# A conv block with a mixture-of-experts tail: a weight load on another queue, choices counted by matmuls, and work around them reordered

## The chip, the cores and the metric

The kernel runs on one core of a Trainium2 chip. The metric is the device time of one execution in microseconds (us). Engines are called PE (matrix), ACT (scalar), DVE (vector), POOL (GpSimd) and SP (sync, which only issues transfers here).

## The reference, cut to what matters

The input is 8 images of 16x16 pixels and 192 channels, 2048 tokens in all. Stage 1 is a layer norm over channels, then 28 correlations of each pixel's unit vector with neighbours along four lines, then a 1x1 convolution over 192 + 28 channels, added to the input. Stage 2 is a layer norm and a top-2 mixture of 8 experts with a capacity:

```python
x = x + _L0_conv_ref(_ln_c(x), conv_w, conv_b)      # features and 28 correlations, 1x1 conv
t = _to_tokens(x)
t = t + _L0_ffn_ref(_ln_t(t), Wg, W1, W2)

# in _L0_ffn_ref, for each of the 2 choices k:
onehot = ik[:, None] == jnp.arange(E)[None, :]
pos = jnp.cumsum(onehot, axis=0) - 1                # a token's place in its expert's list
keep = posk < capacity                              # 307 places
h = jnp.einsum('ecd,edh->ech', xg, W1)
act = h[..., :H] * jax.nn.silu(h[..., H:])
ye = jnp.einsum('ech,ehd->ecd', act, W2)
```

The place of a token in its expert's list depends on all earlier tokens, so stage 2 can start its first expert only when the last token has chosen.

## The kernel before, in words

All orders are written out by hand: each engine has its own block, the engines run their lists in order, and semaphores join them. Stage 1 works on four groups g of 512 tokens (4 tiles of 128). Where the sources below name a call such as `turn_f(2)`, the number is the group.

For a group, in the order of the data: DVE takes mean and variance (`stats`), ACT the square roots (`deviation`), DVE the scales (`scales`), ACT writes normalized features f (`features`), PE transposes them (`turn_f`, lines 980 and 981), ACT copies the result to SBUF (`take_features`), PE forms products of neighbouring pixels (`grams`, lines 1002 and 1003, in two halves), ACT copies them out (`take_gram`), SP stores them to DRAM and reads them back skewed (`gram_round`), POOL picks the 28 correlations (`correlations`, line 454), PE transposes those (`turn_corr`, line 1013), ACT copies them (`take_corr`, tile ct) and PE does the convolution with the router's columns beside it (`conv_features`, line 1026; `conv_rest`, line 1033).

Then DVE has the longest list. `combine` makes router scores (lines 749 and 751), `choose` takes the two best experts and a one-hot tile (lines 775 to 791), `residual` adds the convolution (line 757), `stats_b` takes the second norm's statistics (lines 766 and 769), `find_slots` turns counted places into slots (lines 797 to 806), `row_scales` makes scale and shift of the second norm (lines 811 to 815) and `spots` (lines 822 to 828) makes the tiles from which PE builds a table of tokens by slot (`fill_table`, line 1077). ACT writes the normalized rows (`normed`, line 565), SP stores them to DRAM (`store_rows`, lines 380 and 381) and the residual output (`store_x1`, line 371). Counting is done on PE in `places`: a strictly upper triangular matrix `before` counts within a tile, `ones` counts whole earlier tiles of the group, and `seen`, a running sum that DVE keeps, counts earlier groups.

After group 3 DVE turns the table into row numbers (`indices`, line 840 gives `source`), and POOL, which waits first for `source_ready` and then for all row stores (`rows_out`), gathers the rows of experts 0 and 1 (line 480). Each expert is then a block of matmuls on split operands (lines 1150 to 1158, 1173, 1175), some 18 us, with PE busy nearly throughout. Weights of an expert are four transfers, 1.4 MB: `load_w1` (three, lines 310 to 312) and `load_w2` (line 316). Experts 0 and 1 are loaded by ACT's queue, the others by SP's.

`keep_busy(n, ...)` on PE is a filler: n matmuls of 512 columns whose result nobody reads (line 967). It stands at the start (20), ahead of `turn_corr(0)` (`BUSY_FIRST`, 7), ahead of `turn_corr(3)` (6), between `places(3)` and `fill_table(3)` (`BUSY_TABLE`, 14) and behind `fill_table(3)` (24).

Of the kernel before, what the change touches and what calls it, by code (L numbers as in the profile page):

```python
# [31 lines left out]
BF16 = mybir.dt.bfloat16  # L32
# [90 lines left out]
def metaformer_kernel(nc, x, conv_wt, conv_w, wg, w1, w2, consts, out):  # L123
# [4 lines left out]
    with ExitStack() as ctx:  # L128
# [71 lines left out]
        onehot = sb("onehot", [P, TILES, TOPK, E], BF16)  # L200
        seen = sb("seen", [P, GROUPS, TOPK * E], BF16)
        chosen = sb("chosen", [P, TOPK * E])
# [63 lines left out]
        seen_ready = sem("seen_ready"); shift_ready = sem("shift_ready"); slot_ready = sem("slot_ready")  # L266
# [67 lines left out]
        def _(sp):  # L334
# [75 lines left out]
        def _(pool):  # L410
# [5 lines left out]
            G.memset(seen[:, 0, :], 0.0)  # L416
# [89 lines left out]
        def _(s):  # L506
# [175 lines left out]
        def _(v):  # L682
# [89 lines left out]
            def choose(g):  # L772
# [3 lines left out]
                then(last)  # L776
                for t in range(TILES):
                    last = V.max_index(top_e[:, t, :], top[:, t, :], score[:, t, :])
                then(last)
                if g >= 1:  # L780
                    v.wait_ge(spots_ready, g)
                V.tensor_tensor(onehot[:, :, :, :],
# [4 lines left out]
                if g + 1 < GROUPS:  # L787
                    v.wait_ge(choice_ready, g + 1)
                    then(V.tensor_reduce(chosen[:, :], onehot[:, :, :, :].rearrange("p t k e -> p (k e) t"),
                                         AX_X, ALU.add))  # L790
                    V.tensor_tensor(seen[:, g + 1, :], seen[:, g, :], chosen[:, :], ALU.add).then_inc(seen_ready, 1)

            def find_slots(g):

                picks = slice(g * TILES * TOPK, (g + 1) * TILES * TOPK)
                v.wait_ge(place_done, g + 1)
                then(V.tensor_tensor(place_e[:, :, :],
                                     bank[7][:, 0:TILES * TOPK * E].rearrange("p (n e) -> p n e", e=E),
                                     onehot[:, :, :, :].rearrange("p t k e -> p (t k) e"), ALU.mult))
# [8 lines left out]
            def row_scales(g):  # L808
# [147 lines left out]
        def _(pe):  # L956
# [95 lines left out]
            def places(g):  # L1052

                if g == 0:
                    pe.wait_ge(before_ready, 1)
# [156 lines left out]
```

## Time and profile before

| what | us |
|---|---|
| median of 3 runs (lowest, highest) | 230.23 (229.35, 232.94) |
| the profiled execution, its own time | 229.77 |
| its span in the trace | 228.0 |
| stage 1, to the first gather | about 62.7 |
| eight experts, to the end | about 159 |
| PE busy, share of the span | 205.2, 90% |

### The profile page before, as it was taken

The numbers are of one execution on the slowest core, as the hardware profiler recorded it, in microseconds if no ns is written. First come the engines' busy times: TensorE is split into PE (matmuls) and PEld (weight loads), VectorE is DVE, ScalarE is ACT, GpSimd is POOL, SyncE is SP. The second block draws the span as 40 slices with busy tenths as digits, with TensorE's granted clock in tenths as the row PEclk, the third lists the DMA queues.
The fourth block names the chain that finished last, engine by engine and source line by source line (L and its number), as shares of the span: only waits on it lengthen the run. The fifth ranks groups of instructions, "written<-read, shape, count | busy, mean of one in ns | idle before, by whom it ended". The sixth has DMA issues, their size and how long they took to land.

```text
span 228.0 us, 4487 instructions
## 1 busy us (share of the span) xinstructions
PE 205.2 (90%) x1351; PEld 188.3 (83%) x1351; DVE 160.2 (70%) x509; ACT 128.3 (56%) x320; POOL 118.7 (52%) x130
## 2 busy tenths in 40 slices
PE   7998799869858999999999999999999999999930
PEld 2786699653327999999999999999999999999920
DVE  2674989998704599598598678679778868956520
ACT  2454765374202476587578578577568658745510
POOL 5102212100077154885877787687687683185184
PEclk9999999976795899999999999999999999999995
DMA  6648375879724392494395386288278253034043
GB/s 206 183 123 236 69 204 164 188 195 294 169 73 105 69 289 66 68 286 98 43 262 132 56 252 135 52 175 212 55 139 236 69 52 31 0 36 49 0 46 42
DMA packets 28015, 29.40 MB, mean 129 GB/s; under 512 B 6915, under 2 KB 24544, under 8 KB 28000
## 3 DMA queue, kind: packets, MB, share of 16 engines
q1 hardware_dynamic: 18656, 17.28, 26.6%
q0 software_dynamic: 7680, 9.05, 23.7%
q10 hardware_dynamic: 1664, 2.88, 4.8%
q8 instruction: 7, 0.11, 0.2%
q14 instruction: 8, 0.07, 0.1%
HBM read 19.86 MB, written 9.35 MB: 128 GB/s over the span
## 4 chain that ended last, share of the span: by engine, by line
PE 71%; DVE 11%; DMA 7%; POOL 3%; ACT 3%; issue 2%; SPq 1%; POOLq 0%; DVEq 0%; ACTq 0%
PE low L1173 6%; PE bank L1173 5%; PE first L1157 4%; PE first L1154 4%; PE first L1150 4%; PE first L1158 4%; PE first L1151 4%; PE low L1157 4%; PE low L1158 4%; PE low L1154 4%; PE low L1151 4%; PE low L1150 4%; PE both L1173 3%; PE low L1175 2%; PE bank L1175 2%
## 5 line engine op out<-in xcount | busy, mean ns | idle before, releaser
L500 POOL DMA_INDIRECT out<-y,goal x40 | 65.9, 1648 | 36.6 <-DVE y L933 27.4
L480 POOL DMA_INDIRECT rows<-rows_dram,source x40 | 42.5, 1062 | 36.2 <-DMA rows_dram<-row 18.9
L902 DVE TENSOR_TENSOR al<-act,ah 128x308 fp32r<-128x308 f32 x64 | 30.1, 471 | 1.0
L635 ACT CAST ah<-act 128x308 fp32r<-128x308 f32 x64 | 28.3, 443 | 1.8 <-DVE act L910 1.8
L910 DVE TENSOR_TENSOR act<-low,sil 128x308 f32<-128x308 f32 x32 | 15.3, 479 | 12.8 <-ACT sil L642 12.8
L642 ACT ACTIVATE sil<-first 128x308 f32<-128x308 f32 x32 | 13.7, 428 | 16.7 <-PE first L1158 15.6
L642 ACT ACTIVATE sil<-low 128x308 f32<-128x308 f32 x32 | 13.7, 428 | 14.2 <-PE low L1158 13.3
L910 DVE TENSOR_TENSOR act<-first,sil 128x308 f32<-128x308 f32 x32 | 15.3, 479 | 8.0 <-ACT sil L642 7.2
L1150 PE MATMUL first<-xh_a,hi_a 128*128 128x308 f32 x64 | 20.1, 314 | 0.7 <-ACT xh_a L625 0.7
L1157 PE MATMUL first<-x_b,hi_b 128*128 128x308 f32 x64 | 20.1, 314 | 0.0
L1154 PE MATMUL first<-xl_a,hi_a 128*128 128x308 f32 x64 | 19.9, 312 | 0.1
L1158 PE MATMUL low<-x_b,lo_b 128*128 128x308 f32 x64 | 19.9, 311 | 0.0
L1158 PE MATMUL first<-x_b,lo_b 128*128 128x308 f32 x64 | 19.9, 311 | 0.0
L1157 PE MATMUL low<-x_b,hi_b 128*128 128x308 f32 x64 | 19.9, 311 | 0.0
L1151 PE MATMUL low<-xh_a,lo_a 128*128 128x308 f32 x64 | 19.8, 309 | 0.0
L1151 PE MATMUL first<-xh_a,lo_a 128*128 128x308 f32 x64 | 19.8, 309 | 0.0
L1154 PE MATMUL low<-xl_a,hi_a 128*128 128x308 f32 x64 | 19.8, 309 | 0.0
L1150 PE MATMUL low<-xh_a,hi_a 128*128 128x308 f32 x64 | 19.6, 307 | 0.0
L1173 PE MATMUL low<-w,ah 128*128 128x384 f32 x64 | 19.4, 368 | 0.0
L1173 PE MATMUL bank<-w,ah 128*128 128x384 f32 (+1 forms) x64 | 19.2, 356 | 0.0
L1175 PE MATMUL low<-w,al 128*128 128x192 f32 x64 | 16.0, 251 | 0.0
L967 PE MATMUL first<-ones 128*128 128x512 bf16 x51 | 14.8, 457 | 1.3 <-POOL conv_b L417 1.3
(172 smaller groups left out, 562.3 us busy)
## 6 DMA issues: line engine op xcount, KB each, us to landing
raw_b<-w SPq DMA_DIRECT2D x12, 256.0 KB, 4.1
raw_a<-w SPq DMA_DIRECT2D x6, 512.0 KB, 5.3
raw<-w SPq DMA_DIRECT2D x6, 384.0 KB, 6.1
gram_dram<-gram SPq DMA_DIRECT2D x8, 230.0 KB, 3.2
xt<-x_tokens SPq DMA_DIRECT2D x4, 384.0 KB, 4.4
out<-xt SPq DMA_DIRECT2D x4, 384.0 KB, 5.1
rows_dram<-row SPq DMA_DIRECT2D x3, 386.0 KB, 4.3
raw_b<-w ACTq DMA_DIRECT2D x4, 256.0 KB, 4.2
```

Of the source, the lines that this page charges most:

```text
L480: G.indirect_dma_start(out=rows[b][:, t, :], out_offset=None, in_=rows_dram, in_offset=bass.IndirectOffsetOnAxis(ap=source[:, n:n + 1], ax ...
L500: nc.gpsimd.indirect_dma_start(out=out, out_offset=bass.IndirectOffsetOnAxis(ap=goal[0:m, n:n + 1], axis=0), in_=y[0:m, t, :], in_offset=N ...
L635: nc.scalar.copy(ah[:, j, lo:hi], act[n % 3][:, 0:hi - lo]).then_inc(a_hi, 1)
L642: nc.scalar.activation(sil[n % 2][:, 0:hi - lo], bank[2 * (n % 2) + 1][:, 0:hi - lo], ACT.Silu).then_inc(sil_ready, 1)
L902: V.tensor_tensor(al[:, j, lo:hi], act[n % 3][:, 0:hi - lo], ah[:, j, lo:hi].bitcast(F32), ALU.subtract).then_inc(a_lo, 1)
L910: V.tensor_tensor(act[n % 3][:, 0:hi - lo], bank[2 * (n % 2)][:, 0:hi - lo], sil[n % 2][:, 0:hi - lo], ALU.mult).then_inc(act_ready, 1)
L1150: T.matmul(o, hi_a[b][:, cols], xh_a[:, lo:hi], start=True, stop=False)
L1151: T.matmul(o, lo_a[b][:, cols], xh_a[:, lo:hi], start=False, stop=False)
L1154: T.matmul(o, hi_a[b][:, cols], xl_a[:, lo:hi], start=False, stop=False)
L1157: T.matmul(o, hi_b[b][:, cols], x_b[:, lo:hi], start=False, stop=False)
L1158: mm = T.matmul(o, lo_b[b][:, cols], x_b[:, lo:hi], start=False, stop=True)
L1173: T.matmul(acc, ah[:, j, cols], w_2[b][:, j, :, :].rearrange("p h n -> p (h n)"), start=(j == 0), stop=(j == NH - 1))
```

## The change

Seven things are done. The counting on DVE (`chosen`, `seen`) goes, and `places` counts earlier groups by matmuls of `ones` with the one-hot tiles of those groups, which are now kept apart (one per group); 4, 8 and 12 such matmuls for groups 1, 2 and 3. In `places` they stand first, behind a wait for `slot_ready`, and the `before` matmul stands last. The 7 fillers ahead of `turn_corr(0)` go. On ACT both halves of `take_gram(1)` come ahead of `deviation(3)` and `take_corr(0)`, and `load_w1` of expert 0 comes behind them, directly ahead of `features(2)`. `turn_corr(1)` moves between the halves of `grams(2)`. On ACT `take_corr(3)` moves ahead of `deviation_b(2)`. The weights of expert 1 are issued by SP behind the last row store in place of ACT behind `normed(2)`, and `store_rows(2)` stands ahead of `store_x1(1)`. On DVE the last group takes `residual` and `stats_b` first, then the best scores, then `row_shifts`, and only then `max_index`, the one-hot tile and the rest.

```diff
@@ sync
             store_x1(0)
+            store_rows(2)
             store_x1(1)
-            store_rows(2)
             store_x1(2)
             store_rows(3)
+            load_w1(sp, 1, 1)
+            load_w2(sp, 1, 1)
             store_x1(3)
@@ scalar
             deviation(2)
+            take_gram(1)
+            deviation(3)
+            take_corr(0)
             load_w1(s, 0, 0)
-            take_gram(1, (0,))
-            take_corr(0)
-            deviation(3)
-            take_gram(1, (1,))
             features(2)
...
+            take_corr(3)
             deviation_b(2)
-            take_corr(3)
             normed(2)
-            load_w1(s, 1, 1)
-            load_w2(s, 1, 1)
@@ vector, choose
-                if g + 1 < GROUPS:
-                    v.wait_ge(choice_ready, g + 1)
-                    then(V.tensor_reduce(chosen[:, :], onehot[:, :, :, :].rearrange("p t k e -> p (k e) t"),
-                                         AX_X, ALU.add))
-                    V.tensor_tensor(seen[:, g + 1, :], seen[:, g, :], chosen[:, :], ALU.add).then_inc(seen_ready, 1)
@@ vector, the groups
                 else:
-                    row_scales(g)
+                    residual(g)
+                    stats_b(g)
+                    best_scores(g)
+                    row_shifts(g)
+                    choose(g)
+                    row_gaps(g)
                     find_slots(g)
@@ tensor, places
+                if g >= 1:
+                    pe.wait_ge(slot_ready, g)
+                for p in range(g):
+                    for t in range(TILES):
+                        T.matmul(o, ones[:, :],
+                                 onehots[p][:, t, :, :].rearrange("p k e -> p (k e)").unsqueeze(1).broadcast_to([P, TILES, TOPK * E]),
+                                 start=(p == 0 and t == 0), stop=False, skip_group_check=True)
                 pe.wait_ge(choice_ready, g + 1)
...
                 if g >= 1:
-                    pe.wait_ge(seen_ready, g)
-                    pe.wait_ge(slot_ready, g)
-                T.matmul(o, ones[:, :], seen[:, g, :].unsqueeze(1).broadcast_to([P, TILES, TOPK * E]),
-                         start=False, stop=True).then_inc(place_done, 1)
+                    last = T.matmul(o, before[:, :], picks, start=False, stop=True, skip_group_check=True)
+                last.then_inc(place_done, 1)
@@ tensor, the program
             grams(1)
-            keep_busy(BUSY_FIRST, bank[0])
             turn_corr(0)
             conv_rest(0)
             turn_f(2)
             places(0)
-            grams(2)
+            grams(2, (0,))
             turn_corr(1)
+            grams(2, (1,))
             conv_features(1)
```

On DVE, the last group before, from its scores to its slots (score holds the router's scores, top and top_e the best ones and their experts, xt the tokens, mv_b the second norm's mean and variance):

```order
L751 TENSOR_TENSOR score<-both,part 128x32
L775 MAX top<-score 128x8 x4
L778 MAX_INDEX top_e<-top,score 128x8 x4
L782 TENSOR_TENSOR onehot<-cst,top_e 128x64
L786 TENSOR_TENSOR gap<-top 128x4
L757 SCALAR_TENSOR_TENSOR xt<-both,norm,xt 128x192 x4
L766 BN_STATS stat_b<-xt 128x6 x4
L769 BN_AGGR mv_b<-stat_b 128x2 x4
L811 RECIPROCAL rstd_b<-sd_b 128x4
L812 SCALAR_TENSOR_TENSOR shift_b<-mv_b,rstd_b 128x4
```

And the same place in the changed kernel:

```order
L747 TENSOR_TENSOR score<-both,part 128x32
L753 SCALAR_TENSOR_TENSOR xt<-both,norm,xt 128x192 x4
L762 BN_STATS stat_b<-xt 128x6 x4
L765 BN_AGGR mv_b<-stat_b 128x2 x4
L771 MAX top<-score 128x8 x4
L804 RECIPROCAL rstd_b<-sd_b 128x4
L805 SCALAR_TENSOR_TENSOR shift_b<-mv_b,rstd_b 128x4
L777 MAX_INDEX top_e<-top,score 128x8 x4
L779 TENSOR_TENSOR onehot<-cst,top_e 128x64
L783 TENSOR_TENSOR gap<-top 128x4
```

The one-hot tile, for which `places(3)` on PE waits, moves behind shift_b, for which ACT's `normed(3)` waits.

On PE, the end of stage 1 in the changed kernel (low and bank are PSUM tiles; the filler is `first<-ones` or `low<-ones`):

```order
L1086 MATMUL bank<-tile_e,lane_e 128x40 x8
L1065 MATMUL bank<-onehot,ones 128x64 x12
L1074 MATMUL bank<-onehot,ones 128x48
L1074 MATMUL bank<-onehot,ones 128x32
L1074 MATMUL bank<-onehot,ones 128x16
L1077 MATMUL bank<-onehot,before 128x64
L970 MATMUL low<-ones 128x512 x14
```

Before, the twelve matmuls were not there and one with `seen` stood last; the 14 fillers stood behind the counting in both.

On ACT, the front before, from the second group's features to the third group's:

```order
L513 ACTIVATE len_a<-mv_a 128x4
L310 DMA raw_b<-w 64x1024
L311 DMA raw_b<-w 64x1024
L312 DMA raw_a<-w 128x1024
L549 COPY gram<-low 128x358
L554 COPY ct<-bank 93x512
L512 ACTIVATE sd_a<-mv_a,eps_c 128x4
```

And in the changed kernel:

```order
L548 COPY gram<-low 128x358 x2
L511 ACTIVATE sd_a<-mv_a,eps_c 128x4
L512 ACTIVATE len_a<-mv_a 128x4
L553 COPY ct<-bank 93x512
L308 DMA raw_b<-w 64x1024
L309 DMA raw_b<-w 64x1024
L310 DMA raw_a<-w 128x1024
L523 ACTIVATE f<-xt,shift_a,q_a 128x192 x4
```

The three weight transfers moved from ahead of the copies to a place directly ahead of `features(2)`.

## Rows read from the trace of the kernel before

**Rows 1.** The page, granted TensorE clock in 40 equal slices of the span.

```profile
PEclk9999999976795899999999999999999999999995
```

**Rows 2.** Windows: stretch, length, busy of PE, PEld, DVE, ACT, POOL, clock, DMA share, GB/s.

```profile
18.30:25.80 7.50, 5.16 (x34) 3.53 (x32) 4.14 (x32) 4.12 (x11) 1.68 (x7) 1.00 0.67 178
44.00:49.00 5.00, 2.26 (x13) 1.72 (x12) 4.69 (x23) 2.62 (x6) 0.00 (x0) 1.00 0.71 168
49.00:57.00 8.00, 7.30 (x27) 3.78 (x27) 7.22 (x41) 3.92 (x10) 0.00 (x0) 0.58 1.04 283
59.00:63.00 4.00, 4.00 (x13) 1.53 (x13) 3.22 (x8) 0.00 (x0) 0.31 (x1) 0.57 0.57 109
69.00:77.00 8.00, 7.34 (x32) 6.77 (x31) 3.22 (x7) 2.56 (x6) 5.08 (x5) 0.57 0.40 99
```

**Rows 3.** Timeline of PE, 18 to 26 us: start, duration, then the instruction.

```profile
18.28 1.67 PE L967 MATMUL first<-ones 128*128 128x512 bf16 x7
19.79 0.60 PE L1013 MATMUL bank<-cst,fc 128*93 128x128 f32 x4
21.06 1.67 PE L1033 MATMUL both<-conv_b,ct 93*128 93x208 f32 x8 [0.67 <-ACT ct L554]
23.55 0.30 PE L980 MATMUL first<-cst,f 128*128 128x128 f32 x1 [0.81 <-ACT f L524]
...
25.77 0.57 PE L1002 MATMUL low<-ft_a 128*128 128x179 f32 x2 [0.79 <-ACT rows L538]
```

**Rows 4.** Timelines of ACT and POOL in the same stretch.

```profile
15.09 0.61 ACTq L310 DMA_DIRECT2D raw_b<-w  x1
...
20.43 0.58 ACT L554 COPY ct<-bank 93x512 f32<-93x512 f32 x1 [2.70 <-PE bank L1013]
...
21.54 1.86 ACT L524 ACTIVATE f<-xt,shift_a,q_a 128x192 f32<-128x192 f32 x4
...
18.19 0.89 POOL L454 TENSOR_TENSOR fc<-near,picked 128x28 f32<-128x28 f32 x4 [4.34 <-DMA near<-gram_dram]
```

**Rows 5.** Timeline of DVE, groups 0, 1 and 3 and the indices.

```profile
24.57 0.26 DVE L789 TENSOR_REDUCE chosen<-onehot 128x16 f32<-128x64 bf16 x1
24.87 0.18 DVE L791 TENSOR_TENSOR seen<-seen,chosen 128x16 bf16<-128x16 bf16 x1
...
32.10 0.19 DVE L749 TENSOR_TENSOR part<-both,sd_a 128x32 f32<-128x32 f32 x1 [0.30 <-PE both L1033]
...
49.30 0.18 DVE L749 TENSOR_TENSOR part<-both,sd_a 128x32 f32<-128x32 f32 x1
...
50.16 0.09 DVE L778 MATCH_VALUE_LOAD top_e<-top,score 128x8 f32 x1
...
51.06 1.39 DVE L757 SCALAR_TENSOR_TENSOR xt<-both,norm,xt 128x192 f32<-128x192 f32 x4
...
54.40 0.18 DVE L811 RECIPROCAL rstd_b<-sd_b 128x4 f32<-128x4 f32 x1 [0.36 <-ACT sd_b L558]
...
59.56 0.18 DVE L840 TENSOR_SCALAR source<-filled 128x40 uint32<-128x40 f32 x1
```

**Rows 6.** Timeline of PE, the end of stage 1 and the first expert's rows.

```profile
51.38 5.36 PE L967 MATMUL low<-ones 128*128 128x512 bf16 x14
58.10 1.07 PE L1077 MATMUL bank<-tile_e,lane_e 128*128 128x40 f32 x8 [1.35 <-DVE tile_e L828]
59.01 7.04 PE L967 MATMUL first<-ones 128*128 128x512 bf16 x24
68.55 0.33 PE L1129 MATMUL both<-cst,rows 128*128 128x128 f32 x1 [2.49 <-DMA rows<-rows_dram,source]
```

**Rows 7.** Chain that ended last, in order of time: start, duration, what.

```profile
57.32 4.47 DMA rows_dram<-row
...
62.69 1.19 POOL rows L480
```

**Rows 8.** Source line 381, the row stores' second part, five issues: time to landing.

```profile
DMA to landing us min/median/max: 3.7/4.5/8.3
```

More of the change, by code:

```diff
@@ L199, in metaformer_kernel @@
         top_e = sb("top_e", [P, TILES, 8], U32)
-        onehot = sb("onehot", [P, TILES, TOPK, E], BF16)
-        seen = sb("seen", [P, GROUPS, TOPK * E], BF16)
-        chosen = sb("chosen", [P, TOPK * E])
+        onehots = [sb(f"onehot{g}", [P, TILES, TOPK, E], BF16) for g in range(GROUPS)]
         place_e = sb("place_e", [P, TILES * TOPK, E])
@@ L770, in stats_b, with best_scores @@
                 last.then_inc(var_b, 1)
-            def choose(g):
+            def best_scores(g):
                 for t in range(TILES):
@@ L776, in choose @@
                 then(last)
+            def choose(g):
                 for t in range(TILES):
@@ L984, in turn_f, with grams @@
                 last.then_inc(f_turned, 1)
-            def grams(g):
+            def grams(g, halves=(0, 1)):
                 if g >= 1:
@@ L990, in grams @@
                 fa, fb = ft_a[g], ft_b[g]
-                for t in range(TILES):
+                for t in [2 * h + i for h in halves for i in range(2)]:
                     if g == 0 and t == 0:
@@ L1056, in places @@
                     pe.wait_ge(before_ready, 1)
+                o = bank[7][:, 0:TILES * TOPK * E]
+                if g >= 1:
[5 more added lines that the diff above has]
+                                 start=(p == 0 and t == 0), stop=False, skip_group_check=True)
                 pe.wait_ge(choice_ready, g + 1)
-                o = bank[7][:, 0:TILES * TOPK * E]
-                picks = onehot[:, :, :, :].rearrange("p t k e -> p (t k e)")
-                T.matmul(o, before[:, :], picks, start=True, stop=False)
+                picks = onehots[g][:, :, :, :].rearrange("p t k e -> p (t k e)")
                 for d in range(1, TILES):
                     n = d * TOPK * E
-                    T.matmul(o[:, n:], ones[:, :], picks[:, 0:TILES * TOPK * E - n], start=False, stop=False,
+                    if g == 0 and d == 1:
+                        T.matmul(o, before[:, :], picks, start=True, stop=False, skip_group_check=True)
+                    last = T.matmul(o[:, n:], ones[:, :], picks[:, 0:TILES * TOPK * E - n], start=False, stop=(g == 0 and d == TILES - 1),
                              skip_group_check=True)
                 if g >= 1:
-                    pe.wait_ge(seen_ready, g)
-                    pe.wait_ge(slot_ready, g)
-                T.matmul(o, ones[:, :], seen[:, g, :].unsqueeze(1).broadcast_to([P, TILES, TOPK * E]),
-                         start=False, stop=True).then_inc(place_done, 1)
+                    last = T.matmul(o, before[:, :], picks, start=False, stop=True, skip_group_check=True)
+                last.then_inc(place_done, 1)
             def fill_table(g):
```

27 lines of the change are left out of this document (14 added, 13 removed).

## The prediction

> **What bounds the kernel now.** I read the page first. Its clock row [rows 1] shows PE at full speed except in slices 8 to 10 and 12 to 13 (counted from 0, 5.7 us each), that is from about 49 to 62 us and from 69 to 76 us. Behind that, PE works through eight experts, and nothing in the change touches them. So the change is worth what it moves the moment at which the first expert starts, and nothing else.
>
> The chain of waits [rows 7] says what sets that moment: the last row store is issued at 57.32 and lands 4.47 later, at 61.79, and POOL's first gather starts at 62.69. The other thing that POOL waits for, source, is written at 59.56 + 0.18 = 59.74 [rows 5], 2.05 us before the rows land. The row path is the bound, and the index path is next.
>
> Then the timelines, to see who sets the row path. DVE waits 0.30 us for the convolution of group 1 at 32.10 and goes on from there to 49.30 without a stop [rows 5]: (49.30 - 32.10) / 2 = 8.60 us for a group. PE is close behind it: it waits 0.67, 0.81 and 0.79 us between 18 and 26 us [rows 3]. The windows [rows 2] say what such gaps do. From 44 to 49 us PE was busy for 2.26 of 5.00 us (45%), and the clock then stood at half: a mean of 0.58 over 8 us is 6.7 us at 1.2 GHz. From 18.30 to 25.80 it was busy for 5.16 of 7.50 us (69%) and kept full speed. Two more half-speed stretches lasted 2 x 0.43 x 4.00 = 3.4 us (59 to 63) and 2 x 0.43 x 8.00 = 6.9 us (69 to 77).
>
> **Part 1, the front.** The 7 fillers go; they held PE from 18.28 to 19.79, 1.5 us [rows 3]. The correlations of group 0 are there at 18.19 + 0.89 = 19.08 [rows 4], so their transposes start at about 19.2 in place of 19.79: 0.55 us earlier, and the copy of ct at 19.9 in place of 20.43. But behind this copy now stand three weight issues of 0.61 us [rows 4], 1.85 us in ACT's sequencer, and features(2) comes after them: 19.9 + 1.85 = 21.8 against 21.54 before. The square roots and gram copies that went ahead of ct fit in ACT's 2.70 us wait there. So the next group's features are 0.25 us late, not early. DVE's group 0 does start 0.55 us earlier, and saves the count, but then waits longer for group 1, whose convolution hangs on features(2) and on PE's list from 25.77 on. Splitting the grams around the transposes lets PE work where it had waited for the correlations, which about pays for the 0.25 us. Taken by itself this part is worth 0 at 32.10; bounds are -0.6 (the whole 0.55 arrives) and +0.6 (the issues start late and the weights' transfers slow the gram round trip).
>
> Its side effect is larger. In 18.30 to 25.80 PE loses 1.5 us of filler: 5.16 - 1.5 = 3.65 of 7.50 us, 49%. The nearest row is 45%, after which the clock fell; 69%, where it did not, is far off. I take it that the clock falls between 21 and 26 us. It comes back only once PE has been kept busy, which it is from 26 us on: the half-speed stretches last 3.4 to 6.9 us, and PE's list, which is full there, loses half of that, 1.7 to 3.4 us. I take 2.5. The lower bound is 0 (the clock holds). Group 1 starts on DVE at 34.6 in place of 32.10.
>
> The Trainium skill, page TensorE: Matmul & The Clock Gate, section "HAM oscillation — how this bites in real kernels", gives a practical rule by which only a single idle gap, longer than any that I expect here, drops the clock. By it this term would be 0 and case B below would hold. The trace speaks against it: within 44 to 49 us all idle time together was 2.74 us, and the clock fell. The same page says under "What's actually happening" that the clock is judged at moments that run free of the kernel's start; no row here can show that.
>
> **Part 2, the count.** Reduce and add, 24.57 to 24.96, leave DVE in groups 0, 1 and 2, 0.42 us each with their waits [rows 5]. Group 0's share disappears in the wait for group 1; groups 1 and 2 give 0.84 us. The matmuls that replace them, at most 12 of 64 columns, take a few hundredths each and stand ahead of the wait for the choice: 0, at most +0.4. With take_corr(3) moved up, the convolution of group 3 no longer waits on ACT for DVE's statistics of group 2, so it cannot be what DVE waits for next. So group 3 starts at 49.30 + 2.5 - 0.84 = 50.96.
>
> **Part 3, the last group.** From 49.30 to 50.16 DVE made the scores (two instructions of 0.18, some 0.45 with their waits) and the best four times two (0.41), then index, one-hot and gap up to 51.06 (0.90), then residual and statistics up to 54.40 - 0.36 = 54.04 (2.98) [rows 5]. Now residual and statistics come 0.41 + 0.90 = 1.31 us earlier, and the best scores hide the 0.36 us wait for sd_b. rstd_b and shift_b, two small instructions again, take 0.40, so shift_b comes 0.90 + 0.36 = 1.26 us earlier. But the store also waits for tn_ready, which now follows the index: from the group's start 0.45 + 2.98 + 0.41 + 0.40 + 0.90 + 0.36 (two small ones more) = 5.5 us. The first of the four stores was issued about 1.5 us ahead of the last, which stands at 57.32, and so 6.5 us after the start. The row path gains 1.0 us: last store issued at 57.32 + 1.66 - 1.0 = 58.0, landed at 62.45.
>
> The price is on the index path. The choice of group 3 was ready 51.06 - 49.30 = 1.76 us after the group's start; now it is after 0.45 + 2.98 + 0.41 + 0.40 + 0.90 = 5.14 us. Behind this wait on PE stand the counting, then 14 fillers, then fill_table(3). The fillers hid beside DVE before: 51.38 to 56.74, with the table at 58.10 only because of DVE [rows 6]. Now they start at 50.96 + 5.14 + 0.2 = 56.3, with PE idle for several us ahead of them, so at half speed again. I take the row's own 5.36 us: 61.65. The 24 behind them took 7.04 us with 3.4 at half speed, so one takes 7.04 / (24 + 8) = 0.22 at full speed and 0.44 at half; bounds are 3.1 and 6.2 us. DVE let the table start at 58.10 - 49.30 = 8.8 us after the group's start, now 0.36 less, at 59.4, so the fillers hold it by 2.25 us. From the table's start to source took 59.74 - 58.10 = 1.64: source at 63.3, which is 0.85 us after the rows. The index path becomes the bound, and the gather starts at 63.3 + 0.85 = 64.15 against 62.69: **+1.45 us**.
>
> **Part 4, the weights of expert 1.** Four issues leave ACT, which is not on the path there. They are 1.4 MB, and at 283 GB/s [rows 2] 5 us of traffic that goes from 49 to 57 us to 58 to 64 us. The row stores gain from it, up to 0.8 us (4.47 to the smallest 3.7 of [rows 8]), which counts for nothing while source is later. Expert 1's weights are first read in the blocks of expert 0, after the gather. store_x1(3) is issued 2.1 us later and waited for long after. On SP's queue nothing urgent stands behind them: 0, with -0.8 and +1 as bounds. The swap of store_rows(2) and store_x1(1) is 0.
>
> **Part 5, the first expert.** PE's 24 fillers end at 59.01 + 7.04 = 66.05 and the rows come at 68.55 [rows 6], a gap of 2.5 us, and the clock fell for 6.9 us [rows 2]. Now the fillers end at 61.65 + 0.9 + 24 x 0.22 = 67.8, and the rows come 1.45 later at 70.0: a gap of 2.2 us. I take no change; if the clock stays full, half of 6.9 less PE's idle time in it, 3.1 us, is saved.
>
> The sum is 1.45 us on the profiled 229.77, 231.2. Its likely errors lean down (the store and the fillers at their lower ends), so I say **230.9**, 0.7 us over the median of 230.23. A measurement of this kernel can tell about 2% (4.6 us) from no change.
>
> **Rivals.** B: the clock holds in the front. For it: 49% is a little more than 45%. Then group 3 starts at 48.46, the rows land at 59.95, the fillers run from 53.8 to 59.2, source is at 60.8, the gather at 61.65: -1.05, 228.7.
>
> C, faster by over 2%: as B, and the fillers run at full speed, so that the rows bind (gather 60.8, -1.9), and the first expert keeps full speed (-3.1): 224.8. Against it: PE idles some 3 us ahead of the fillers in any case, as the choice comes 5.14 - 1.76 us later.
>
> D, slower by over 2%: the 1.4 MB on SP's queue sit between the last stores and the gather and share the engines with both. It decides once the last row store takes the 8.3 us that one took [rows 8] in place of 4.47: rows at 66.3, gather at 67.15, +4.5, with gathers slowed on top by about 1 us: 235.3. Against it: the stores are issued first, and the load that shared their time before is gone.
>
> E: the index path hides again, as the fillers end early and the store landing is the bound, while the clock costs 2.5: rows at 62.45, gather 63.3, +0.6, 230.4. It lies inside the forecast's range.
>
> **How the numbers follow.** Forecast with E 0.62 (own range 229.3 to 233.0), B 0.22, C 0.08, D 0.05, clock losses in the front and again in the first expert that add to over 4.6 us 0.03. The range runs from 227.8, below B, to 233.2 and leaves about 0.17 out. Faster 0.09, same 0.83, slower 0.08.
>
> **What would show it.** The clock row falls in slices 4 and 5; DVE's wait at group 1 is about 3 us and not 0.30; reduce and add are gone; from the group 3 start to shift_b it is 4.2 us and not 5.3; POOL's first gather is released by DVE's source and no longer by the row store; the 14 fillers end after DVE's tile_e. The forecast is wrong if the front keeps full speed, or if the rows still bind the gather.

## The result, and the profile after

The changed kernel took 232.63 us (median of 11 executions, 230.52 to 233.70), the kernel before 229.88 us on the same chip (11 executions, 229.16 to 232.94). The ratio is 1.0123 with a 95% interval of 1.0084 to 1.0163: slower by 1.2%, within the 2% that was forecast as "no change". Run again in a later set of runs, the same file gave 230.53 us against 230.15 and a ratio of 1.0054 (1.0019 to 1.0089). The point forecast was 230.9, a rise of 0.7 us over the kernel before; the rise of the medians is 2.75 us here and 0.4 there. Two sets of the experiments ran on chips where the kernel before itself took 240.2 to 240.6 us; their times are compared only within the set. Times given below are medians over all executions, while ratios leave out the executions that ran over 1.5% above the fastest of their kernel, so a ratio can differ from the quotient of the two medians.

The profiled execution of the first set is its longest, 233.70 us with a span of 231.1. That of the second took 230.68 us with a span of 227.9. Both are read here, since a good part of what sets the changed kernel's time differs from execution to execution.

The granted clock in the page of the changed kernel, first profile:

```profile
PEclk9999589995697699999999999999999999999995
```

Against [rows 1] there is a new dip in slices 4 and 5, so it came where it was forecast. The windows of the same profile:

```profile
18.30:25.80 7.50, 4.55 (x29) 3.58 (x27) 5.43 (x35) 3.80 (x10) 1.47 (x6) 0.89 0.82 219
...
44.00:49.00 5.00, 3.74 (x35) 2.80 (x34) 4.70 (x29) 0.77 (x2) 0.89 (x4) 1.00 0.61 162
49.00:57.00 8.00, 4.93 (x32) 4.00 (x30) 6.61 (x32) 4.27 (x10) 0.00 (x0) 0.65 0.69 146
59.00:63.00 4.00, 4.00 (x15) 1.72 (x13) 2.46 (x8) 1.54 (x3) 0.00 (x0) 0.67 0.75 176
69.00:77.00 8.00, 4.62 (x18) 3.85 (x17) 2.15 (x4) 0.86 (x2) 6.17 (x7) 0.68 0.51 125
```

In [rows 2] the first of these stretches was at full speed, with 5.16 us busy. The 4.55 us here include matmuls stretched by the lower clock. The PE timeline shows where the time went idle:

```profile
20.24 1.67 PE L1036 MATMUL both<-conv_b,ct 93*128 93x208 f32 x8 [0.67 <-ACT ct L553]
23.57 0.30 PE L983 MATMUL first<-cst,f 128*128 128x128 f32 x1 [1.66 <-ACT f L523]
...
26.19 0.96 PE L1005 MATMUL low<-ft_a 128*128 128x179 f32 x2 [1.02 <-ACT rows L537]
```

The convolution starts 0.82 us earlier than in [rows 3] (20.24 against 21.06), but the features' transposes start at 23.57, as they did at 23.55. So the wait for `f` grew from 0.81 to 1.66 us. ACT's timeline says why:

```profile
19.61 0.55 ACTq L308 DMA_DIRECT2D raw_b<-w  x1
19.62 0.57 ACT L553 COPY ct<-bank 93x512 f32<-93x512 f32 x1
20.20 0.61 ACTq L309 DMA_DIRECT2D raw_b<-w  x1
20.84 0.60 ACTq L310 DMA_DIRECT2D raw_a<-w  x1
21.56 1.86 ACT L523 ACTIVATE f<-xt,shift_a,q_a 128x192 f32<-128x192 f32 x4 [1.38 <-issue]
```

The copy of `ct` ends at 20.19, and then two weight issues still stand in ACT's sequencer. ACT's datapath idles for 1.38 us, which the profile puts down to "issue". The DVE timeline at the starts of groups 1 and 3 and at the end of stage 1:

```profile
34.47 0.19 DVE L745 TENSOR_TENSOR part<-both,sd_a 128x32 f32<-128x32 f32 x1 [1.85 <-PE both L1036]
...
50.35 0.18 DVE L804 RECIPROCAL rstd_b<-sd_b 128x4 f32<-128x4 f32 x1 [0.90 <-ACT sd_b L557]
...
63.90 0.32 DVE L833 TENSOR_REDUCE filled<-bank 128x40 f32<-128x160 f32 x1 [2.34 <-PE bank L1086]
64.26 0.18 DVE L836 TENSOR_SCALAR source<-filled 128x40 uint32<-128x40 f32 x1
```

Group 1 starts 2.37 us later than in [rows 5], and `source` comes 4.7 us later. DVE waited 1.85 us at the group's start, and 2.03 us more ahead of it for the square root `sd_b`. PE, at the end of stage 1:

```profile
58.17 4.89 PE L970 MATMUL low<-ones 128*128 128x512 bf16 x14
62.71 1.15 PE L1086 MATMUL bank<-tile_e,lane_e 128*128 128x40 f32 x8
...
71.78 0.44 PE L1138 MATMUL both<-cst,rows 128*128 128x128 f32 x1 [2.72 <-DMA rows<-rows_dram,source]
```

The fillers of [rows 6] now start 6.8 us later, and the table follows them. DVE finished `tile_e` at about 61.5, before the fillers ended. The chain of waits in the profile runs this way:

```profile
58.36 4.70 PE low L970 x14
63.06 0.81 PE bank L1086 x8
...
63.90 0.33 DVE filled L833
...
64.26 0.18 DVE source L836
...
64.79 0.67 issue
65.46 1.58 POOL rows L479
```

In [rows 7] the row store stood ahead of POOL's gather. Here the profile puts the fillers, the table and `source` there. But the last row store was issued at 59.81:

```profile
59.81 0.48 SPq L379 DMA_DIRECT2D rows_dram<-row  x1
...
DMA to landing us min/median/max: 4.4/4.4/4.4
```

It landed at 64.21, only 0.23 us ahead of `source` (64.44), and the chain alone does not say which of the two held the gather. The gather starts 1.02 us after `source` and 1.25 us after the landing. In the profiles in which `source` is clearly last, POOL starts 0.30 to 0.33 us after it; in those in which the store is clearly last, 1.2 us after its landing (0.9 in the kernel before). By these distances it was the row store's landing that held the gather in this execution, and the index path, ready for a gather at about 64.75, was 0.7 us earlier. Behind the first rows on PE nothing changed: 231.1 - 71.78 = 159.3 us to the end, against 228.0 - 68.55 = 159.5 before.

A second delay is in this profile and not in the other. The chain between 34 and 50 us has this line:

```profile
38.52 6.32 DMA gram_dram<-gram
```

The gram store of group 3 landed in 6.32 us behind the row store issued at 37.35. Its convolution's copy `ct` was therefore late (49.47 to 50.05), and with `take_corr(3)` moved ahead of `deviation_b(2)` it held the square root: that is the wait of 0.90 us at 50.35.

The chain of the second profile of the same file:

```profile
55.54 4.94 PE low L970 x14
60.48 0.81 PE bank L1086 x8
...
61.67 0.20 DVE source L836
61.87 0.28 issue
62.15 1.70 POOL rows L479
63.85 0.31 issue
64.16 1.28 POOL rows L479
...
65.74 2.91 DMA rows<-rows_dram,source
...
68.70 0.33 PE both L1138
```

Here the gather starts at 62.15, 0.54 us *earlier* than before, and PE's first rows come at 68.70 against 68.55. The last row store had landed at 60.6, so in this execution it was `source`, behind the fillers, that held the gather, 0.30 us after it was written. The front dip is shorter, one of 3.4 us in place of 6.8, and group 1 starts at 32.79.

Stage 1 of the profiles side by side, each number from the timelines of DVE, SP, POOL and PE (the rows of experiments included):

```
                     features(2) group1 group3 | from group 3: row store  gather  PE rows
                                               |               issued
before                  21.54    32.10  49.30  |      8.02     13.39   19.25
changed, first          21.56    34.47  52.93  |      6.88     12.53   18.85
changed, second         20.91    32.79  50.11  |      6.88     12.04   18.59
fillers7_back           22.71    36.81  53.73  |      6.89     12.93   19.46
before_no_fillers7      20.70    30.91  48.22  |      8.01     13.13   19.02
w1_early                20.02    31.45  48.80  |      6.89     11.70   18.99
w1_early_repeat         19.52    32.86  49.99  |      6.89     12.59   19.12
table_fillers_split     20.96    33.86  50.95  |      6.89     11.88   18.67
last_group_old          20.76    33.50  51.00  |      8.01     12.92   20.18
weights_act             20.91    33.49  51.07  |      6.89     12.61   18.66
```

One part of the difference is in no trace. The time of an execution less its span was 1.81 us for the kernel before (median of 29, all of the second set), 2.71 for the changed kernel in the first set (11) and 2.03 in the second (12). In the second set, over the executions that the ratio counts, the median went from 229.64 to 230.53 us and the median span from 227.75 to 228.35. So some 0.9 of the 2.75 us of the first set, and 0.2 of the 0.9 us of the second, lie outside the span.

### The profile page after: what moved, and what is told of

It reads as the page before. It is cut to its first block, busy times and chain, and to the rows that moved or that the text cites. A ratio compares the mean times of both kernels' runs of the same rounds, so it can differ in the third digit from the quotient of the medians.

```text
span 231.1 us, 4506 instructions
## 1 busy us (share of the span) xinstructions
PE 206.4 (89%) x1364; PEld 191.1 (83%) x1364; DVE 159.6 (69%) x503; ACT 128.1 (55%) x320; POOL 119.0 (51%) x129
## 4 chain that ended last, share of the span: by engine, by line
PE 79%; DMA 5%; DVE 4%; POOL 4%; ACT 4%; issue 2%; ACTq 1%; SPq 0%; DVEq 0%; POOLq 0%
PE low L1182 5%; PE bank L1182 5%; PE first L1166 4%; PE first L1163 4%; PE first L1159 4%; PE first L1167 4%; PE first L1160 4%; PE low L1166 4%; PE low L1167 4%; PE low L1159 4%; PE low L1160 4%; PE low L1163 4%; PE first L970 3%; PE both L1182 3%; DMA gram_dram<-gram 3%; PE low L1005 3%
## 5 line engine op out<-in xcount | busy, mean ns | idle before, releaser
L499 POOL DMA_INDIRECT out<-y,goal x40 | 66.0, 1651 | 36.6 <-DVE y L936 27.4
L1184 PE MATMUL bank<-w,al 128*128 128x192 f32 (+1 forms) x64 | 16.0, 250 | 0.0
```

The lines of the kernel that those rows point to most:

```text
L499: nc.gpsimd.indirect_dma_start(out=out, out_offset=bass.IndirectOffsetOnAxis(ap=goal[0:m, n:n + 1], axis=0), in_=y[0:m, t, :], in_offset=N ...
L1184: mm = T.matmul(acc[:, 0:C], al[:, j, cols], w_2[b][:, j, 0, :], start=False, stop=(j == NH - 1), skip_group_check=True)
```

## The experiments

**The front.** The prediction had the clock fall because the 7 fillers go. The rival: it falls because of the wait for `features(2)`. Two kernels bring the fillers back, or take them from the kernel before.

```diff
             grams(1)
+            keep_busy(7, bank[0])
             turn_corr(0)
```

> The changed kernel with the 7 fillers ahead of turn_corr(0) put back. Theory (the clock): without them PE falls to 1.2 GHz in the front (the trace shows half speed from 24.0 to 30.8 us) and DVE's group 1 starts 2.4 us late. With them the clock row has no dip in slices 4 and 5, group 1 starts near 32.3 us and the kernel takes about 230.2, ratio to the kernel before 1.001. Rival 1 (the fillers only cost): PE gets 1.5 us more work in front of turn_corr(0), the clock does the same as without, ratio 1.013 to 1.018. Rival 2 (the late features alone delay group 1): ratio stays at 1.012.

```diff
             grams(1)
-            keep_busy(BUSY_FIRST, bank[0])
             turn_corr(0)
```

> The kernel before with only the 7 fillers taken out, all orders as before. Clock theory: PE's busy share in the front falls as in the changed kernel, the clock dips, group 1 starts 2 us late, ratio 1.008 to 1.012. Rival (the fillers are dead weight, and the change lost its time by the moved weight load on ACT or by the gram stores): group 1 starts up to 0.5 us earlier, ratio 0.998 to 1.000.

The times, 239.4 and 239.3 us against 240.56 (ratios 1.0027, 0.9977 to 1.0077, and 1.0003, 0.995 to 1.0056), settle nothing. The profiles do. First the changed kernel with the fillers back, its clock row:

```profile
PEclk9999569995697999799999999999999999999995
```

Its PE timeline and its window have

```profile
24.71 0.45 PE L983 MATMUL first<-cst,f 128*128 128x128 f32 x1 [1.65 <-ACT f L523]
...
18.30:25.80 7.50, 5.17 (x28) 3.75 (x27) 4.15 (x31) 3.19 (x8) 1.02 (x4) 0.86 0.75 204
```

The dip stays and is longer than any other in the front, 10.2 us from 23.7 on, though PE was busy for 5.17 us of that stretch; the kernel before, with 5.16, kept full speed there [rows 2]. The kernel before without its fillers has no front dip:

```profile
PEclk9999999957776999999999999999999999999995
```

and its group 1 starts at 30.91, earlier than the 32.10 of [rows 5]. Its expected dip did not come, and neither did the cure expected of the fillers in the changed kernel. So in these two profiles the fillers did not decide it. What the two kernels with a dip share is the wait of 1.65 us for `f`. Each is a single execution, and a run further below shows that one file can fall in one execution and not in another.

**The weight issues.** `load_w1` of expert 0 goes back directly behind `deviation(2)`, all else stays changed:

```diff
             deviation(2)
+            load_w1(s, 0, 0)
             take_gram(1)
             deviation(3)
             take_corr(0)
-            load_w1(s, 0, 0)
             features(2)
```

> The changed kernel with only load_w1 of expert 0 moved back on ACT to directly behind deviation(2), ahead of the gram copies; fillers still gone. New theory: the three issues ahead of features(2) (1.9 us of ACT's sequencer) leave PE idle 1.7 us ahead of turn_f(2), and that idle time drops the clock, not the missing fillers. Expected: features(2) starts 1.4 us earlier (near 20.2), the clock row has no dip in slices 4 and 5, group 1 starts near 31.0 in place of 34.5, and the kernel gains 2 to 3.5 us against the changed one: ratio 1.000 or below. Rival (the missing fillers drop the clock): the dip stays, at most 1.4 us come out, ratio 1.006 to 1.010.

In the same set the changed kernel itself ran, and gave the second profile above:

> The changed kernel itself, on the chip on which the runs of this call are made, as their reference. Both theories expect a ratio near 1.012 to the kernel before, as measured first; if it is near 1.000 here, the part runs are to be judged by this chip's own number.

This kernel took 228.96 us (227.87 to 231.46, 12 executions) against 230.53 of the changed and 230.15 of the one before: ratio to before 0.9973 (0.9934 to 1.0012), where the changed kernel has 1.0054. It is 1.6 us faster than the changed kernel, less than the 2 to 3.5 us expected: those were reckoned from the first profile's dip of 6.8 us, and in this set the changed kernel's was 3.4. The clock row of this kernel:

```profile
PEclk9999999995995999999999999999999999999995
```

Its PE timeline, and its window of the front:

```profile
22.03 0.30 PE L983 MATMUL first<-cst,f 128*128 128x128 f32 x1 [0.18 <-ACT f L523]
...
18.30:25.80 7.50, 5.17 (x33) 4.03 (x32) 4.95 (x33) 5.76 (x14) 1.44 (x6) 1.00 0.59 170
```

The wait for `f` is 0.18 us where it was 1.65. PE is busy for 5.17 us without any filler, because the work has moved into the stretch. The clock stays full, and group 1 starts at 31.45. From the group's start to the rows on PE nothing is gained (18.99 us), so the gain is all from the front: 68.70 - 67.79 = 0.91 us at PE's first rows. The gain is not only in one profile. Of the 12 executions of this kernel 6 had a mean granted clock of 0.955 or more; of the 30 of the three kernels in this set that issue the weights directly ahead of `features(2)` (the changed kernel and the two experiments devb_first and weights_act below), 2 had. The edit moves the issues on ACT and the traffic of the weights together; what the traffic does by itself was not tried.

The same file once more, on another chip:

> The kernel of the run w1_early again, as the reference of the three below. Expected as then: ratio 0.995 to 0.999, no dip of the clock in slices 4 and 5. Rival: the gain was the chip's scatter, ratio 1.002 or more.

```profile
PEclk9999799965979997999999999799799999999995
```

238.74 us against 240.22 (0.9958, 0.9897 to 1.0019), and in this execution the clock fell at 26.1 all the same, although features(2) was at 19.52. It fell during a wait of 1.58 us for the correlations (`fc`, until 26.80), which was 1.02 us in the first profile of the same file. So the place of the weight issues doesn't decide the dip by itself. It takes one long wait away; another, for the transfer of the grams to memory and back, can still be long in one execution and not in the next. The longest of these waits stands in a profile further below (early_last_old, 2.37 us until 28.12), and there too the clock fell.

**Fillers with the early issues.** `load_w1` early, and the 7 fillers back:

> As w1_early, with the 7 fillers ahead of turn_corr(0) back. If the late features alone had dropped the clock, the fillers have nothing left to save: they start the transposes of group 0's correlations 0.5 to 0.9 us later, and group 1 with them: 0.3 to 0.9 us slower than w1_early. Rival (the fillers hold the clock in those executions in which it falls at another moment): 0.3 us or more faster, above all fewer long runs.

240.98 us, 0.9988 (0.9925 to 1.0051), beside 0.9958 for w1_early_repeat in the same set; no front dip in its profile. features(2) comes at 20.85, but group 1 at 31.48, as in w1_early (31.45), so the expected delay of 0.3 to 0.9 us did not reach it in this profile. No gain from the fillers is seen, and the times can't tell a small loss.

**The place of `take_corr(3)`.** The 0.90 us wait for `sd_b`, seen in the first profile, might be a steady cost of the changed order:

```diff
-            take_corr(3)
             deviation_b(2)
+            take_corr(3)
```

> The changed kernel with deviation_b(2) ahead of take_corr(3) on ACT, as before. Theory: DVE waited 0.90 us for sd_b of group 2, because ACT stood waiting for the transposed correlations; with the old order this wait goes and group 3 starts up to 0.9 us earlier, minus what conv_rest(3) then comes late: 0.3 to 0.9 us out, ratio 0.002 to 0.004 below the changed kernel. Rival (the convolution of group 3 then is what DVE waits for): no gain.

230.66 us, ratio 1.0049 (1.001 to 1.0088), the same as the changed kernel beside it (1.0054), and not the 0.002 to 0.004 below it that was expected. The second profile of the changed kernel has no such wait either. The wait of 0.90 us belonged to the late gram store of one execution.

**The fillers before the table.** Seven of the 14 go ahead of the wait for the choice and 5 stay behind it, so there are two fewer in all:

```diff
             fill_table(2)
+            keep_busy(7, bank[2])
             places(3)
-            keep_busy(BUSY_TABLE, bank[2])
+            keep_busy(5, bank[2])
             fill_table(3)
```

> The changed kernel with 7 fillers ahead of places(3) and 5 behind, in place of 14 behind. In the changed kernel's trace source is written at 64.44 and the last row store lands at 64.21, so the two paths are equal. Theory: the index path gains up to 2.3 us, but the rows bind at once behind it, so only about 0.2 us come out: ratio 1.010 to 1.013. Rival (the fillers alone hold the gather, as predicted): 1.5 us or more come out, ratio 1.006 or less.

239.42 us, 0.9986 (0.9935 to 1.0037). That is in the range of the rival (1.006 or less), but the changed kernel, with 1.0054 in another set, is in it too, and it did not run in this one. So the profile has to decide. From the start of group 3, `source` is written after 10.92 us in place of 11.74 in the changed kernel's second profile, but the gather starts after 11.88 against 12.04 and the rows are on PE after 18.67 against 18.59. So the 0.8 us by which the index path is shorter don't reach the gather. The last row store landed at 61.5 here and the gather started 1.3 us later, at 62.83. With the early weight issues added:

> As w1_early, with 7 fillers ahead of places(3) and 5 behind in place of 14 behind. In w1_early the table's matmuls start right behind the fillers at 58.35, DVE's tile_e being done near 57.4, and source is written at 60.08, the rows landing at about the same time. Theory: source comes up to 0.9 us earlier, but the rows bind, so 0 to 0.3 us come out: ratio within 0.002 of w1_early. Rival (prediction: the fillers hold the gather alone): 0.9 us or more, ratio 0.004 lower.

240.59 us, 1.0024 (0.9964 to 1.0084), where w1_early_repeat has 0.9958; the intervals overlap. `source` comes after 10.28 us, the gather after 11.90, the rows after 18.39. The chain of waits of this profile says what holds the gather now:

```profile
55.57 3.76 DMA rows_dram<-row
...
59.36 1.21 issue
60.57 1.58 POOL rows L479
```

It is the row store's landing again, as in [rows 7]. The two paths are within 1 us of each other, and shortening one alone brings little.

**The order of the last group.** DVE's old order (scores and choice first):

```diff
+                    best_scores(g)
+                    choose(g)
                     residual(g)
                     stats_b(g)
-                    best_scores(g)
                     row_shifts(g)
-                    choose(g)
```

> The changed kernel with the last group in its old order on DVE (best scores, index and one-hot ahead of residual and statistics); all else as changed. Theory: the row path loses the 1.0 us that the new order gave, the index path gains 2.3 us or more and hides again, so the rows bind: about +0.7 us, ratio 1.014 to 1.017. Rival (the new order costs as much as it gives, because it puts the choice late): same as changed or faster, ratio 1.008 to 1.012.

242.8 us (6 executions, of which the ratio rests on 3), 1.0119 (1.0025 to 1.0213). It is the only kernel of its set whose interval lies above 1. The last row store is issued 8.01 us after the group's start as in the kernel before, against 6.89, and PE's rows come after 20.18 us. Most of that is not the store: the gather starts after 12.92 us, inside the 11.70 to 12.93 of the profiles with the new order, and from there to PE's rows it takes 7.26 us. With the early issues:

> As w1_early, with the last group in its old order on DVE. No dip of the clock blurs it. Theory: the last row store is issued 1.0 us later after group 3's start (7.9 in place of 6.9), the fillers hide again beside DVE, the rows bind: 0.5 to 1.0 us slower than w1_early. Rival: what the rows gained the fillers took, equal to w1_early.

240.39 us, 0.9944 (0.9884 to 1.0004), where w1_early_repeat has 0.9958: not the 0.5 to 1.0 us slower that was expected. The store is again 1.1 us later (8.03), and the gather starts after 13.15 us, but the rows come after 19.01, as in w1_early with the new order (18.99 and 19.12). In its profile the clock fell at 27.4, in the wait of 2.37 us told of above. So the new order puts the store 1.1 us earlier in every profile; whether that reaches the end isn't settled, since the set without the early issues hints at yes and the one with them says no.

**The weights of expert 1.** ACT issues them again behind `normed(2)`, and `store_rows(2)` stands behind `store_x1(1)`:

```diff
@@ sync
             store_x1(0)
-            store_rows(2)
             store_x1(1)
+            store_rows(2)
...
-            load_w1(sp, 1, 1)
-            load_w2(sp, 1, 1)
@@ scalar
             normed(2)
+            load_w1(s, 1, 1)
+            load_w2(s, 1, 1)
```

> The changed kernel with expert 1's weights issued by ACT behind normed(2) again and store_rows(2) behind store_x1(1). Theory (as predicted): worth nothing or up to 0.8 us worse, as 1.4 MB share the time of the last row stores again while source binds as well: ratio within 0.003 of the changed kernel. Rival (loads behind the stores slow the first gathers, which took 6.3 us from first issue to PE in place of 5.9): 0.5 us or more better.

231.97 us (6 executions), 1.0107 (1.0045 to 1.0169), beside the changed kernel's 1.0054 (1.0019 to 1.0089): a ratio 0.005 higher, where 0.003 at most was expected. The intervals overlap. The second parts of the last group's two row stores land in 2.5 and 3.6 us in the changed kernel's second profile (3.5 and 4.4 in its first) and in 3.9 and 4.5 here, so the stores gain up to 1 us from the move. First rows on PE: 18.66 after the group's start against 18.59. The medians differ by 1.4 us in favour of the changed kernel, but part of that is the front: the dip of this profile is 6.8 us long and that beside it 3.4. What the move and the swap of the stores are worth is not shown to be more than nothing; that they cost anything is not seen.

## Why the prediction was right or wrong

The forecast, no change within 2% and a little slower, held: 1.2% and 0.5% were measured, 0.3% was said. That is in part luck. The rise of 2.75 us in the first set is four times the 0.7 forecast, and the range was wide enough to hold it. The steps that led to it were of mixed quality, and errors went against each other.

**The reading of the bound** held. From PE's first rows to the end it is 159.5 us before, 159.3 and 159.2 in the two profiles of the changed kernel, 159.0 in w1_early. Only the start of the first expert moves.

**The front: right place, wrong cause, and the size right in one profile of two.** The clock fell in slices 4 and 5, and group 1 started at 34.47 where 34.6 was said. In the second profile it was 32.79, as the half-speed stretch was 3.4 us in place of 6.8; the first profile is the longest execution of its set. The step that failed is the one by which PE loses 1.5 us of filler, is busy for 49%, and the clock falls for that. With the fillers back the share is that of the kernel before (5.17 and 5.16 of 7.50 us) and the clock falls, and in the kernel before without them (4.92 us) it doesn't, in the one profile taken of each. What I had worked out beside it, three issues of 0.61 us ahead of features(2), I had costed as 0.25 us late, by comparing 21.8 with 21.54. It came at 21.56 and 20.91. I had left out that PE arrives at this point earlier than before (convolution at 20.24 and 19.58), so that what was no delay for ACT was a doubled wait for PE. The busy share of the window, on which I built, does not tell these kernels apart. The longest single wait does, in the front. PE's waits in 18.3 to 25.8 us together are 2.27 us before (0.67, 0.81, 0.79 [rows 3]), 2.26 in w1_early (0.51, 0.67, 0.18, 0.70, 0.20) and 2.32 with the fillers back (0.67, 1.65). Only the last fell. Of the fourteen profiles of this study, nine show a fall between 22 and 28 us, and PE's longest wait there is 1.48 to 2.37 us in these; in the other five it is 0.81 to 1.06 us. That is a correlation over runs which differ in other things too: in seven of the nine the three weight issues stand directly ahead of `features(2)`, and in the other two the wait was for `fc`. In the kernel before, the fall at 49.0 also followed a long wait:

```profile
46.71 1.67 PE L1033 MATMUL both<-conv_b,ct 93*128 93x208 f32 x8 [2.12 <-ACT ct L554]
```

But a long wait does not suffice. Between experts, before_no_fillers7 has a wait of 2.34 us until 89.63, with PE busy for 1.66 us of the 4.00 from 87 to 91, and keeps full speed from 84 to 96 us; fillers7_back has one of 2.40 us until 94.73 at the same place in the program, and its clock fell at 95.3. What exactly drops the clock stays open. Shown is that the early weight issues take the wait for `f` from 1.65 to 0.18 us.

The Trainium skill, page TensorE: Matmul & The Clock Gate, section "HAM oscillation — how this bites in real kernels", looks at single idle gaps. In direction the runs side with it: in the front the longest gap went with the fall (1.48 us and more against 1.06 and less), and the busy share did not (5.17 of 7.50 us with a fall and without). In size they don't: the clock fell with gaps of 1.48 to 2.37 us, which by the page are too short. The rule taken as it stands would have given no dip (case B), and the dip in both profiles of the changed kernel speaks against it. The page's remark under "What's actually happening", that the chip's moments of judging run free of the kernel's start, is not tested by these runs; that one file falls in one execution and not in the other (w1_early and its repeat) is compatible with it, but the wait for `fc` differed too, 1.02 and 1.58 us. It is compatible as well that of two waits nearly equal, 2.34 and 2.40 us, only one was followed by a fall.

**The count: over-sized.** 0.42 us each in groups 1 and 2 were said. Group 2 to 3 took 8.35 us in the second profile in place of 8.60, a gain of 0.25. Group 1 to 2 took 8.97, a loss of 0.37, since DVE now waits 0.28 us for the counting matmuls (`place_e`), and the chain of this profile reaches group 2 through PE, POOL and a gram store of 4.45 us, no longer through DVE. I had costed the matmuls that replace the reduction at "0, at most +0.4", and the upper end is nearer. The group start of 50.96 that I forecast was 50.11 and 52.93.

**The last group.** The row path's gain of 1.0 us was right: 6.88 against 8.02 us, 1.14. That the index path takes over, for which the prediction said that rows still binding would prove it wrong, is true of the second profile and not of the first, in which the row store's landing held the gather, as shown above. In the profiles of w1_early, table_fillers_split and early_table_split the landing is the last again, by 0.1 us and more. So the two paths came out nearly level, where `source` had been put 0.85 us behind the rows. One term was mis-sized for both: 0.85 us to the gather from whichever is last. From `source` it is 0.3 us, from the landing 1.2 in the changed kernel. The other terms were mostly too large. From the group's start the fillers begin after 5.24 us (5.34 said) and end after 10.13 and 10.37 (10.69 said): they took 4.89 and 5.12 us, not the 5.36 of [rows 6]. From their end to `source` it is 1.4 us (1.64 said). The gather starts 12.53 and 12.04 us behind the group's start, where 13.2 was said (64.15 - 50.96). The kernel before needed 13.39, so the last group's reordering does pay up to here, 0.9 and 1.35 us, where I had it at 0.2.

**What took it back.** The gather itself, costed at no change. From the gather's start to PE's rows it was 68.55 - 62.69 = 5.86 us before, and it is 6.32, 6.55 and, in w1_early, 7.29. The first two indirect issues take 1.70 and 1.28 us in place of 1.19 and 0.96 (second profile), while between 60 and 66 us the DMA share is 1.02 in place of 0.29. The profile's window of the changed kernel, second profile:

```profile
60.00:66.00 6.00, 6.00 (x34) 3.27 (x32) 3.22 (x8) 0.00 (x0) 3.23 (x3) 1.00 1.02 277
```

and of the kernel before:

```profile
60.00:66.00 6.00, 6.00 (x22) 2.28 (x20) 2.49 (x5) 0.00 (x0) 2.70 (x3) 0.78 0.29 70
```

That is rival D at a small scale: the 1.4 MB of weights sit in the gather's stretch, and the stretch is 0.5 to 0.7 us longer in these two. With the weights on ACT's queue again it was 6.05 us. The size differs much from profile to profile. In the eleven profiles in which SP issues these weights the stretch is 5.86 to 7.29 us, mostly 6.3 to 7.1; in the three in which ACT does, it is 5.86, 5.89 and 6.05. A part comes back at the stores, which I had said would gain "up to 0.8" and count for nothing.

**The sum.** In the second profile the front costs 0.69 at group 1 and 0.81 at group 3, the last group gives back 0.66 at PE's rows, and the two leave 0.15 us: the spans of the two profiles are equal. The median spans of the set differ by 0.6 us. In the first, a longer dip and a late gram store leave 3.2 us. What lies outside the span adds 0.2 to 0.9 us. Why it is larger and more scattered in the changed kernel (1.8 to 3.0 us, before 1.7 to 2.1 in the second set) no experiment was made for, and it stays open. Open too is how often each version falls in the front, since each profile shows one execution.

## What to carry to other kernels

A weight issue held ACT's sequencer for 0.55 to 0.61 us here. Three of them ahead of an operation that another engine waits for are a wait on that other engine, and the time by which *that* engine arrives decides its length. The wait for `f` was 1.65 us with them there and 0.18 without. Work this out for the waiting engine before saying that the issuing engine is hardly later. Where a clock dip follows, look at the single waits ahead of it and not only at the busy share, which was the same here with a dip and without. Neither decided it alone. Test the suspected cause from both sides, in the new kernel and in the old one; one side alone had looked convincing here. Take each kernel's profile more than once before you believe it, as the same file fell in one and not in the other.

Filler matmuls behind a wait move with it: when the choice was made some 3 us later after the group's start, the fillers queued behind it came 3 us later, and the table 1 us later.

Where two paths lead to one start, measure the distance from each to it in profiles in which that one is clearly last. Which of them held the start can then be told even where the chain names the other.

The best version measured keeps all of the change but for `load_w1`, 228.96 us, 0.9973 (0.9934 to 1.0012) of the kernel before: not shown faster than it, but 0.7% below the changed kernel in the same set, and the two intervals (1.0019 to 1.0089 for the changed kernel) don't meet.

## What the runs showed of the hardware

The same file gets a different clock in different executions. Of the 29 executions of the kernel before in the second set, 10 had a mean granted clock of 0.955 or more and a median span of 227.0 us, and 9 had one below 0.94 and 230.5 us. The changed kernel was at 0.955 or more in none of 12, w1_early in 6 of 12 (226.0 us). The difference of 3.5 us between the two groups is the larger part of the spread of the kernel before (spans of 225.7 to 230.7 us), and a profile shows one draw from it.

Half-speed stretches in the profiles last about 3.4, 6.8 or 10.2 us (from 49.0, 59.2 and 69.5 us on before; from 24.1, 51.4 and 71.9 after).

On ACT a weight issue held the sequencer for 0.55 to 0.61 us, and the activation behind the last of three started 1.38 us after the datapath had become free.

The first indirect gather's issue on POOL took 1.19 us in the kernel before and 1.58 and 1.70 in the two profiles of the changed one, with 1.4 MB of weight loads in flight; the second took 0.96, and 0.96 and 1.28; from the third on nearly all took 0.95 us in all three.
